# Third layer of a four-layer graph network: a third of the source tiles fetched from DRAM by indirect DMA

## The reference, cut to what matters

```python
def _L2_gnn_ref(x, edge_index, edge_attr, ...):          # third layer
    src, dst = (edge_index[0], edge_index[1])
    e_h = jax.nn.silu(edge_attr @ edge_W1 + edge_b1)
    e_w = jax.nn.sigmoid(e_h @ edge_W2 + edge_b2)
    x_agg = jax.nn.silu(x[src] @ agg_W + agg_b) * e_w
    out = jax.ops.segment_sum(x_agg, dst, num_segments=n)
    cnt = jax.ops.segment_sum(jnp.ones((dst.shape[0],), x.dtype), dst, num_segments=n)
    out = out / jnp.maximum(cnt, 1.0)[:, None]
    ...
def _L3_gnn_ref(...):                                    # fourth layer
    msg = (node_states[src] + rel_vec) @ W_msg.T + b_msg
    agg = jax.ops.segment_sum(msg, dst, num_segments=n_nodes)
    agg = agg / jnp.maximum(deg, 1.0)[:, None]
    return node_states @ W_self.T + b_self + agg
x = _layernorm(x + _L0_gnn_ref(...)); x = _layernorm(x + _L1_gnn_ref(...))
x = _layernorm(x + _L2_gnn_ref(...)); x = _layernorm(x + _L3_gnn_ref(...))
```

## Time and profile before

| | before |
|---|---|
| median of three runs | 1165.83 us |
| profiled execution: own time / span | 1165.81 / 1164.0 us |
| granted TensorE clock, mean | 0.954 |
| busy of the span: TensorE | 1036.2 us (89%) |
| VectorE / ScalarE / GpSimd | 933.2 (80%) / 645.8 (55%) / 77.9 us (7%) |
| gather products of the third layer, L2151 | 1950, 126.3 us busy |
| scatter products of the third layer, L2163 | 1300 records for 650 products, 168.3 us busy |

### The profile page before, as it was taken

One profiled execution on the slowest core, in us unless ns is written; L12 is line 12 of the kernel. 1 busy time (PEld: TensorE's weight loads), 2 busy tenths in 40 slices (PEclk: granted clock), 3 DMA queues, 4 the chain that ended last, 5 costly groups with the idle time before them and its releaser, 6 DMA issues.

```text
span 1164.0 us, 28509 instructions
## 1 busy us (share of the span) xinstructions
PE 1036.2 (89%) x10937; PEld 902.0 (77%) x10937; DVE 933.2 (80%) x2140; ACT 645.8 (55%) x1324; POOL 77.9 (7%) x117
## 2 busy tenths in 40 slices
PE   4798978899999999959999997799999999818994
PEld 3344566899999999947776777599999999717784
DVE  6767999889899899879888988877777776695445
ACT  3466856455555554579888985533333333353663
POOL 4403040000000000000000000000000000030000
PEclk9898999899999999979999998899999999958998
DMA  6000020544444444123334331222222221123882
GB/s 149 1 1 1 4 64 5 179 148 149 146 150 148 150 153 145 60 73 100 124 125 131 121 114 44 75 86 79 89 75 90 86 78 60 69 72 118 249 229 56
DMA packets 70762, 116.26 MB, mean 100 GB/s; under 512 B 8443, under 2 KB 47302, under 8 KB 70396
## 3 DMA queue, kind: packets, MB, share of 16 engines
q1 hardware_dynamic: 70201, 113.56, 31.6%
q10 hardware_dynamic: 426, 0.85, 0.3%
HBM read 91.14 MB, written 23.24 MB: 98 GB/s over the span
## 4 chain that ended last, share of the span: by engine, by line
PE 78%; DVE 12%; ACT 4%; DMA 2%; issue 2%; POOL 0%; POOLq 0%; SPq 0%; DVEq 0%; ACTq 0%
PE PS L1979 13%; PE PS L2163 13%; PE PS L1967 10%; PE PS L2151 9%; PE PS L2202 7%; PE PS L2084 6%; PE PS L2052 3%; PE PS L2059 3%; ACT X L1024 2%; PE PS L1805 2%; PE PS L1818 2%; DMA adj_d<-ring 2%; DVE vo L1331 2%; DVE ring L1327 2%; PE PS L1882 1%
## 5 line engine op out<-in xcount | busy, mean ns | idle before, releaser
L948 ACT CAST vo<-XT 128x768 f32<-128x768 bf16 (+1 forms) x218 | 180.6, 829 | 237.9 <-PE PS L2163 123.1
L1979 PE MATMUL PS<-vo 128*128 128x133 f32 x1300 | 175.9, 284 | 1.0 <-DVE vo L1433 1.0
L2163 PE MATMUL PS<-vo 128*128 128x128 f32 x1300 | 168.3, 279 | 0.8 <-DVE vo L1699 0.8
L1979 PEld LDWEIGHTS PS<-vo 128*128 128x128 f32 x1300 | 157.2, 191 | 1.1 <-issue 1.1
L2163 PEld LDWEIGHTS PS<-vo 128*128 128x128 f32 x1300 | 153.6, 191 | 1.0 <-ACT vo L948 1.0
L1967 PE MATMUL PS<-kp,ring 128*128 128x132 bf16 x1950 | 146.1, 220 | 3.3 <-DVE ring L1301 1.8
L1699 DVE TENSOR_TENSOR vo<-PS,EWS 128x768 f32<-128x768 f32 (+1 forms) x109 | 103.7, 951 | 50.2 <-PE PS L2151 49.9
L1967 PEld LDWEIGHTS PS<-kp,ring 128*128 128x128 bf16 x1950 | 125.3, 97 | 5.5 <-DVE ring L1301 1.9
L2151 PE MATMUL PS<-kp,ring 128*128 128x128 bf16 x1950 | 126.3, 219 | 0.8 <-ACT big L1105 0.8
L1085 ACT CAST ring<-PS 128x512 bf16<-128x512 f32 (+1 forms) x175 | 116.7, 672 | 10.1 <-DMA adj_d<-ring 10.0
L1309 DVE TENSOR_TENSOR XT<-iotab,XT 128x768 bf16<-128x768 bf16 (+1 forms) x218 | 122.1, 560 | 0.0
(11 more groups left out here) (318 smaller groups left out, 1851.7 us busy)
## 6 DMA issues: line engine op xcount, KB each, us to landing
ring<-rows_d SPq DMA_DIRECT2D x146, 416.0 KB, 3.9
adj_d<-ring SPq DMA_DIRECT2D x100, 128.0 KB, 1.8
adj_d<-ring SPq DMA_DIRECT2D x75, 96.0 KB, 1.8
ring<-adj_d SPq DMA_DIRECT2D x11, 640.0 KB, 4.6
vo<-adj_d SPq DMA_DIRECT2D x9, 640.0 KB, 4.0
vo<-adj_d SPq DMA_DIRECT2D x8, 480.0 KB, 4.8
ring<-adj_d SPq DMA_DIRECT2D x7, 480.0 KB, 4.7
big<-rows_d SPq DMA_DIRECT2D x4, 416.0 KB, 7.6
```

The lines of the kernel that those rows point to most:

```text
L948: C.copy(ohd[:, k % 3, 0:n, :], ohb[:, k % 3, 0:n, :]).then_inc(hots_wide, 1)
L1979: T.matmul(bank(6 + b % 2)[:, 0:VW], ohd[:, k % 3, i, :], vals[:, k % 3, i, :], start=j == 0, stop=j == JN - 1).then_inc(scattered, 1)
L2163: T.matmul(bank(6 + q % 2)[:, (b % 4) * P:(b % 4 + 1) * P], vals[:, k % 3, i, 0:F], ohd[:, k % 3, i, :], start=j == 0, stop=j == JN - 1).t ...
```

## The change

In each full batch of six the first four tiles are "near" and gathered by products as before; the last two are "far" (FAR = 2). The silu rows T1 are stored to a DRAM table by SP in seven DMAs, one for each four blocks, after the first two row loads. GpSimd computes for every slot the row of its source node from the tile number and the slot's position (six operations over 128x650), then for every far tile issues one indirect DMA: 128 rows of 512 bytes, one for each slot, straight into the place of `vals` that the scatter reads. ScalarE scales the two far tiles in place by their weights, and the scatter waits for that too. 216 tiles are far. The gathers now need one bank for a batch, and have four of them.

The fourth layer's bias moves: count x b_msg to ScalarE, one row of blocks for each of the first 25 batches; b_self to one VectorE add over all 3200 columns at tile 24 of the widening. Semaphores for stores and loads of the adjacency are merged (adj_io, crel_io), and SP's first adjacency load waits also for the last far tiles.

```diff
+FAR = 2
+GBUF = 4
+    def near(k):
+        return batch(k)[:BT - FAR] if len(batch(k)) == BT else batch(k)
+    def far(k):
+        return batch(k)[len(near(k)):]
...
-            with sp.If(general == 1):
-                sp.wait_ge(silu2, BANKS)
-                sp.dma_start(tab[2].rearrange("(b p) f -> p b f", p=P), T1).then_inc(g_tab, 16)
             for h in range(NU):
                 if h >= RBUF:
                     sp.wait_ge(hots_src, 2 * NU + h - RBUF + 1)
                 row_load(0, h, row_in[0])
-            sp.wait_ge(gathered_up, 2 * NT)
+                if h == RBUF - 1:
+                    for i in range(BANKS):
+                        sp.wait_ge(silu2, i + 1)
+                        sp.dma_start(tab[2].rearrange("(b p) f -> p b f", p=P)[:, nodes(i), :], T1[:, nodes(i), :]).then_inc(rows2_out, 16)
+            sp.wait_ge(gathered_up, NT + near_until(NT))
+            sp.wait_ge(far_ready, far_batches(NBATCH - 1))
...
-            for i in range(BANKS):
-                pool.wait_ge(gathered_up, NT + NT * (i + 1) // (BANKS + 2))
-                G.tensor_tensor(bias3[:, s, :], cnt[:, s]..., bmsg..., ALU.mult).then_inc(bias3_step, 1)
-                G.tensor_tensor(bias3[:, s, :], bias3[:, s, :], bself..., ALU.add).then_inc(bias3_step, 1)
+            pool.wait_ge(rel_mm, BANKS * NB)
+            pool.wait_ge(ohs_ready, BANKS * JN)
+            G.iota(far_row, pattern=[[0, NB], [P, JN]], base=P, channel_multiplier=0).then_inc(far_step, 1)
...
+            pool.wait_ge(rows2_out, 16 * BANKS)
+            for k in range(NBATCH):
+                if len(far(k)):
+                    if k >= 3:
+                        pool.wait_ge(scattered, NT + batch_end(k - 3))
+                    for t in far(k):
+                        G.indirect_dma_start(vals[:, k % 3, t - BT * k, 0:F], None, tab[2],
+                                             bass.IndirectOffsetOnAxis(ap=far_row[:, t:t + 1], axis=0)).then_inc(far_in[k % 3], 16)
...
+            act.wait_ge(rows2_out, 16 * BANKS)
...
+            def far_scaled(k):
+                if len(far(k)):
+                    act.wait_ge(far_in[k % 3], 16 * FAR * far_uses(k))
+                    for t in far(k):
+                        v = vals[:, k % 3, t - BT * k, 0:F]
+                        o = C.activation(v, v, ACT.Copy, scale=EWS[:, t:t + 1])
+                    o.then_inc(far_ready, 1)
             for k in range(NBATCH):
                 hots_widened(k, 1)
+                if k:
+                    far_scaled(k - 1)
+                if k < NB:
+                    o = C.activation(bias3[:, k, :], bmsg[:, :], ACT.Copy, scale=cnt[:, k:k + 1])
...
+            far_scaled(NBATCH - 1)
...
-                dve.wait_ge(gathered_up, NT + batch_end(k))
-                V.tensor_tensor(vals[:, k % 3, 0:n, 0:F]..., gathered(k, 0, F), EWS..., ALU.mult).then_inc(vals_ready, 1)
+                t = near(k)
+                n = len(t)
+                dve.wait_ge(gathered_up, NT + near_until(t[-1] + 1))
+                V.tensor_tensor(vals[:, k % 3, 0:n, 0:F], bank(k % GBUF)[:, 0:n * F]..., EWS..., ALU.mult).then_inc(vals_ready, 1)
...
+                if s == 24:
+                    loose(V.tensor_tensor(NX[:, :, :], NX[:, :, :], bself[:, :].unsqueeze(1).to_broadcast([P, NB, F]), ALU.add))
...
             def gather2(k):
-                if k >= 3:
-                    pe.wait_ge(vals_ready, NBATCH + k - 2)
-                for i, t in enumerate(batch(k)):
+                if k >= GBUF:
+                    pe.wait_ge(vals_ready, NBATCH + k - GBUF + 1)
+                for i, t in enumerate(near(k)):
...
             def scatter2(k):
                 pe.wait_ge(hots_wide, NBATCH + k + 1)
                 pe.wait_ge(vals_ready, NBATCH + k + 1)
+                if len(far(k)):
+                    pe.wait_ge(far_ready, far_batches(k))
```

More of the change, by code:

```diff
@@ L120, in batch, with near_until, far_batches, far_uses @@
         return range(BT * k, min(BT * k + BT, NT))
+    def near(k):
+        return batch(k)[:BT - FAR] if len(batch(k)) == BT else batch(k)
+    def far(k):
+        return batch(k)[len(near(k)):]
+    def near_until(t):
+        return sum(1 for k in range(NBATCH) for n in near(k) if n < t)
+    def far_batches(k):
+        return sum(1 for n in range(k + 1) if len(far(n)))
+    def far_uses(k):
+        return sum(1 for n in range(k % 3, k + 1, 3) if len(far(n)))
     def source(t):
@@ L215, in gnn_kernel @@
         CT = NREL * 4
+        far_row = ring[:, RBUF * HW:RBUF * HW + 2 * NT].bitcast(i32)
+        far_sum = ring[:, RBUF * HW + 2 * NT:RBUF * HW + 4 * NT].bitcast(fp32)
         ohs = ring[:, 0:3 * (2 * OH1 + CT)].rearrange("p (r n) -> p r n", r=3)
@@ L469, in gnn_kernel @@
         identr_ready = sem("identr_ready")
-        adj_out = [sem(f"adj_out{n}") for n in range(ABUF)]
+        adj_io = [sem(f"adj_io{n}") for n in range(ABUF)]
         applied = sem("applied")
@@ L475, in gnn_kernel @@
         crelT_cp = sem("crelT_cp")
-        crel_out = [sem(f"crel_out{n}") for n in range(2)]
+        crel_io = [sem(f"crel_io{n}") for n in range(2)]
         ag_ready = sem("ag_ready")
@@ L492, in gnn_kernel @@
         bias3_step = sem("bias3_step")
-        adj_in = [sem(f"adj_in{n}") for n in range(CBUF)]
-        crel_in = [sem(f"crel_in{n}") for n in range(2)]
+        rows2_out = sem("rows2_out")
+        far_step = sem("far_step")
+        far_in = [sem(f"far_in{n}") for n in range(3)]
+        far_ready = sem("far_ready")
         wide_act = sem("wide_act")
@@ L545, in batch_end, with adj_stored, crel_stored @@
             return min(BT * (k + 1), NT)
+        def adj_stored(r):
+            return 16 * len(range(r, BANKS * NB, ABUF))
+        def crel_stored(r):
+            return 16 * len(range(r, BANKS, 2))
         def on_act(s):
@@ L788, in _ @@
             with pool.If(general == 1):
[L789 removed]
+                pool.wait_ge(g_tab, 64)
                 sums_gather(3)
@@ L1099, in _ @@
             split(1, T1, lambda i: act.wait_ge(silu2, i + 1))
-            with act.If(general == 1):
-                act.wait_ge(g_tab, 64)
+            act.wait_ge(rows2_out, 16 * BANKS)
             for i in range(BANKS):
@@ L1298, in edge_hots @@
                 if h >= OBUF:
-                    dve.wait_ge(gathered_up, turn * NT + (h - OBUF + 1) * HT)
+                    past = (h - OBUF + 1) * HT
+                    dve.wait_ge(gathered_up, NT + near_until(past) if turn else past)
                 raw = rows0 if turn == 0 and h < RBUF else rows
@@ L1735, in _ @@
             copy_xt(2)
-            dve.wait_ge(bias3_step, 2 * BANKS)
+            dve.wait_ge(bias3_step, 1)
             norm_wait(dve, 4)
```

52 lines of the change are left out of this document (28 added, 24 removed).

## The result

| | before | changed |
|---|---|---|
| median (lowest to highest) | 1166.01 us (1164.48 to 1167.81) | 1211.51 us (1206.98 to 1216.44, 4 runs) |
| profiled execution, span | 1165.81, 1164.0 | 1206.98, 1205.2 |
| first scatter to the last full batch's, 108 periods | 256.3 us | 297.3 us |
| a period, median / mean | 2.40 / 2.37 us | 2.53 / 2.75 us |
| VectorE / ScalarE / GpSimd busy | 933.2 / 645.8 / 77.9 us | 905.7 / 717.4 / 280.2 us |

The changed kernel takes 1.0385 times as long (95% interval 1.0359 to 1.041): 45 us slower, where 16 us faster was forecast. The profiled execution is the quickest of the four, so the two traces differ by 41.2 us. The loop holds 41.0 of them.

The account below looks back on a forecast made before the run. TensorE's own work was taken to bound the third layer's edge loop, at 2.40 us a batch. With a ring of 2.23 us: 1165.8 - 18.4 + 2.0 (fourth layer) = 1149.4 us, range 1130 to 1196.

Parts of the forecast that it names:

- the price d of an issue: Third layer's loop: GpSimd spends 1.06 us on each indirect DMA, 2.12 us for a batch's two; bounds 0.32 and 1.33.
- the second rival: Third layer's loop: GpSimd's queue becomes the bound, 2.66 us a batch at d = 1.33, 1196 us in all; chance 0.30.
- the landing L: Third layer's loop: a far tile's DMA lands 1.9 us after its issue ends; ends 1.5 and 3.3 us.
- the ring's length over three: Third layer's loop: buffer wait, two issues, landing, scaling and scatter sum to 6.70 us; over three buffers, 2.23 us a batch.
- TensorE 2.06 us a batch: Third layer's loop: 12 gather products take 0.67 us, scatter 1.39; 0.34 less a batch, at most 37 us over 108 batches.
- ScalarE's two scalings, 0.87 us: Third layer's loop: ScalarE scales two far tiles in 0.87 us; its batch of 1.57 to 1.96 us costs nothing.
- Clock left at full: Third layer's loop: TensorE's waits of about 0.17 us a batch are too small to lower its granted clock.
- The lock beside VectorE: Third layer's loop, rival: GpSimd's issues stop during VectorE's source hots, losing 31 us; period 2.41, 1169 us; chance 0.12.
- Bias rows on ScalarE, index operations, the table's store: Bias rows in the third layer's loop, index operations and store before it: all hidden beside other work, costing nothing.
- Fourth layer, 2.0 us: VectorE's second bias addition makes TensorE wait 1.2 us, plus up to 1.6 for a lower clock; 2.0 taken.
- the hidden ring: Third layer's loop, rival: the ring falls under 2.06 us, TensorE bounds again, 1131 us in all; chance 0.20.
- my own ring: Third layer's loop, the main forecast: a ring of 2.1 to 2.36 us a batch sets the period; chance 0.38.

Follow-up runs that it names:

- experiment 1: The changed kernel with one far tile in each batch of six instead of two, and three gather places; 1157.03 us, 0.9897 of the kernel before.
- experiment 2: The changed kernel with six buffers of their own for the far tiles, so GpSimd waits for the batch six before; 1187.47 us, 1.0171 of before.
- experiment 5: The changed kernel with six far-tile buffers and plain 64 KB DMAs from GpSimd, choice of rows left out; 1133.67 us, 0.9716 of before.
- experiment 4: The changed kernel without most of the third layer's 416 KB row loads, hots built from stale rows; 1188.41 us, 1.0176 of before.
- experiment 6: One far tile a batch, with b_self added by GpSimd again instead of VectorE's second addition; 1153.92 us, 0.9886 of the kernel before.
- 2, 1, 2: The changed kernel with two, one, two far tiles in turn, six buffers and b_self on GpSimd; 1146.53 us, 0.9828 of before.
- the plain DMAs from GpSimd: The changed kernel, three buffers, with plain DMAs issued by GpSimd for the indirect ones, choice of rows left out; 1157.44 us, 0.9915 of before.
- 1, 2: The changed kernel with one and two far tiles in turn, six buffers and b_self on GpSimd; 1149.24 us, 0.9838 of before.
- the plain DMAs from ScalarE: The changed kernel, three buffers, with plain DMAs issued by ScalarE's queue for the indirect ones, choice of rows left out; 1152.59 us, 0.9862 of before.

## Why the prediction was wrong

**The step that failed is the price d of an issue, as a pitch.** I took 1.06 us and let the next start at once: 2.12 us a batch in the queue. Measured: 0.95 us and then 0.30 us in which nothing is shown, 1.25 us from start to start, 2.50 us a batch. The single duration was even too high; the gap behind it was not in the sum at all. I had put the point from which the queue decides at d = 1.20. The pitch of 1.25 lies just past it, so the second rival came true. Its formula gives 0.10 x 108 = 11 us more; against the loop as it was, 2.50 x 108 = 270 us are 14 more than 256.3. No row of before shows such a gap (the 25 copies of the earlier trace rows have 0.4 us of "issue" between them all), but nothing excluded it either, and a queue that issues without waiting has to be priced from start to start. The Trainium skill (DMA: Bandwidth & Descriptors, section on the anatomy of one DMA on the gpsimd path) calls the making of descriptors small; here GpSimd spends 0.95 us on an issue of 64 KB in 128 rows, and two of them with their gaps bound the loop, so the measurement decides against it. From the start of an issue to its landing the runs have 0.95 + 1.99 = 2.94 us, close to my own 2.96 and not to the 2.15 that the prediction worked out from the same section.

**The second step that failed is the landing L as one value.** I gave it 1.9 us, and took the ring's length over three as a period. The median is 2.0 us to the semaphore, so the value was right, and so was the ring at its median: 0.26 + 2.20 + 2.0 + 0.69 + 0.14 + 1.56 = 6.85 us by the rows above, 2.28 a batch where I had 2.23. But a ring with a fixed number of buffers pays for the late ones. Three periods of 2.50 us leave 7.5 - 4.85 = 2.65 us for a landing, an estimate from the same terms, and 27 of 105 took more than 2.8; with one far tile (experiment 1) it is 3.4 us by the same working. Once the queue was the bound I would have forecast 1165.8 + 14 + 2 = 1182 us; of the rest, 27 us of the profiled execution's loop, 20 are stalls from that spread and 7 the loop's ends (six buffers gave back 25 and 24 us of loop in experiments 2 and 5, though in experiment 2 six more issues before the loop are part of it). Row loads bring most of the spread (experiment 4: 17.7 us). The code loads' part wasn't tried alone. My own upper end for L, 3.3 us, came from those same row loads; they themselves hardly suffer, 3.7 us in the median where they took 3.6.

The other steps:
- *TensorE 2.06 us a batch:* right. 2.06 median in experiment 5, with 224 us for 108 batches; the 37 us at most came out as 32, since 108 x 2.40 is 259 and the loop was 256.3.
- *ScalarE's two scalings, 0.87 us:* 0.69 us as a pair, median 392 ns of one. Right that it costs nothing: ScalarE has 161 of 300 us.
- *Clock left at full:* wrong. Six stretches of 3.4 us in the loop have a granted clock of 0.50, the lower level, where before had none; the one shown above cost 1.3 us. In experiment 5 the one stretch below full is at the loop's start, and none lies behind it, so they go with the stalls.
- *The lock beside VectorE:* there, but small. 17 issues in which the source hots (L1359, the line I suspected) start 0.2 to 0.46 us behind the issue's own start end 0.12 us after them, as the lock quoted in the prediction would have it; that is 2.8 us in all, where my rival had 31, since the two seldom meet so and 32 other meetings left the issue at 0.95 us. A second hold-up I hadn't thought of costs more: 21 issues end 0.82 us after a VectorE instruction with two inputs from SBUF, mostly the destination hots (L1367), 5.1 us. All that is above 0.945 us sums to 9.7 us over 216 issues. That sorting is by overlap in the records; no run took VectorE's work away.
- *Bias rows on ScalarE, index operations, the table's store:* nothing, as forecast; the first six DMAs are out by 736.4. The loop starts 1.5 us late.
- *Fourth layer, 2.0 us:* the wait was right, the clock went the other way. Waits of TensorE for widened tiles from the fourth layer's start:
```profile
PE PS L2265 <- DVE adjf_r L1807: 3.3, 2, 2.2
```
```profile
1101.57 3.48 DVE L1810 TENSOR_TENSOR big<-big,X 128x3200 f32<-128x3200 f32 x1
...
1105.66 0.47 PE L2265 MATMUL PS<-adjf_r,xh_r 128*128 128x512 f32 x1 [2.22 <-DVE adjf_r L1807]
...
1115.41 0.47 PE L2265 MATMUL PS<-adjf_r,xh_r 128*128 128x512 f32 x1 [1.04 <-DVE adjf_r L1807]
```
```profile
1104.00:1108.00 4.00, 2.34 (x10) 1.98 (x11) 2.67 (x5) 0.93 (x3) 0.00 (x0) 1.00 0.30 88
```
The second addition makes TensorE wait 1.04 us, where I had 1.2. But the clock, which in the earlier trace rows fell to 0.51 after the first wait, stays at 1.00 here after a wait of 2.2 us (2.1 there). From the first product to the end the eleven traces fall into four cases: 104.8 us with one addition and no fall of the clock (experiment 6, and 2, 1, 2), 106.2 with two and no fall (the change, experiments 2, 4, 5 and the plain DMAs from GpSimd), 106.5 with one and a fall (before, and 1, 2), 107.5 to 107.6 with two and a fall (experiment 1, and the plain DMAs from ScalarE). So the addition costs 1.0 to 1.4 us and the fall 1.3 to 1.7. The changed kernel's trace has the one and lacks the other. What brings the fall about wasn't tested. The traces sort by one thing: the granted clock had last risen to full 3.3 to 3.8 us before the fourth layer's first product in the four with a fall, and 4.2 to 4.9 us before it in the seven without.

**The chances.** The queue, the ring and the lock all exist, and only the hidden ring does not; I gave the queue 0.30 and my own ring 0.38 with d only 0.14 us under the point of decision, between bounds of 0.32 and 1.33. The range ended at 1196 because I let only one thing go wrong at a time: queue or ring. The truth is both together, 270 us of queue plus 27 us of stalls and ends, and neither alone explains 1211.5. A slip besides: a ring of 2.1 us gives 1165.8 - 0.30 x 108 + 2 = 1135 us, not 1137.

## What to carry to other kernels

Price an engine's queue from start to start, not by the duration of one instruction, and ask first how many issues a loop needs for the time it has: 216 x 1.25 us did not fit into 256, 180 x 1.25 = 225 us did. A prefetch ring's length over its depth holds only for the median landing; give it buffers for the late ones (here six in place of three, 25 us), above all where large loads share the DMA engines. Where the work can be split in any ratio, take the ratio at which both engines are just busy, instead of moving as much as possible.

## What was not expected of the hardware

- An indirect DMA of 128 rows of 512 bytes costs GpSimd 0.94 us at least and 0.30 us more before the next; a plain one of the same 64 KB 0.53 at least, and in the run with six buffers three went in 1.59 us without a gap.
- An indirect issue that meets VectorE's addition of two SBUF operands ends 0.8 us after it: 4.14 and 3.34 us in place of 0.94. A plain issue from GpSimd isn't held up by such an instruction, 31 times out of 31 in experiment 5.
- A wait of 2.1 or 2.2 us on TensorE at the same place of the fourth layer was followed by 3.4 us at a granted clock of 0.50 in four traces of eleven, and by none in the seven others.
